# A selective state-space scan on one core: ten columns a state, and the end state's squares moved to VectorE

## What is computed

```
def step(h, inp):
    dA_t, dB_t, x_t, C_t, t = inp
    h = h * dA_t + dB_t * x_t[:, :, None]
    nrm = jnp.sqrt(jnp.sum(h * h, axis=(1, 2), keepdims=True))
    fac = jnp.minimum(20.0 / (nrm + 1e-08), 1.0)
    h = jnp.where(t % 10 == 0, h * fac, h)
    y = jnp.einsum('bdn,bn->bd', h, C_t) + D_param * x_t
    return (h, y)
```

## Time and profile before

| | us |
|---|---|
| median of 3 runs | 1531.29 (1530.69 to 1533.32) |
| the profiled execution, its own time | 1536.68 |
| span of its instructions in the profile | 1534.8 |
| DVE busy / POOL busy / ACT busy / PE busy in the span | 1255.2 / 939.6 / 1121.2 / 1455.1 |

### The profile page before, as it was taken

One profiled execution on the slowest core, in us unless ns is written; L12 is line 12 of the kernel. 1 busy time (PEld: TensorE's weight loads), 2 busy tenths in 40 slices (PEclk: granted clock), 3 DMA queues, 4 the chain that ended last, 5 costly groups with the idle time before them and its releaser, 6 DMA issues.

```text
span 1534.8 us, 25461 instructions
## 1 busy us (share of the span) xinstructions
PE 1455.1 (95%) x6902; PEld 1020.6 (66%) x6902; DVE 1255.2 (82%) x2526; ACT 1121.2 (73%) x2618; POOL 939.6 (61%) x956
## 2 busy tenths in 40 slices
PE   6999999999979999999999999999999998999998
PEld 5555555555467777777777777777666666677776
DVE  6685566745479999999999999999999998788884
ACT  4444455455999999999999999999999964334243
POOL 0224313432269999999999999999999997400000
PEclk9999999999999999999999999999999999999999
DMA  8215437453757667666666666666545447466420
GB/s 269 83 49 176 131 103 198 139 178 115 233 137 208 169 165 188 168 172 167 172 165 181 177 162 181 157 173 172 133 111 112 95 105 224 116 221 193 150 84 28
DMA packets 231557, 236.28 MB, mean 154 GB/s; under 512 B 46040, under 2 KB 197272, under 8 KB 231416
## 3 DMA queue, kind: packets, MB, share of 16 engines
q1 hardware_dynamic: 230472, 233.34, 54.4%
q10 hardware_dynamic: 944, 1.31, 0.2%
HBM read 136.31 MB, written 98.56 MB: 153 GB/s over the span
## 4 chain that ended last, share of the span: by engine, by line
DVE 35%; POOL 14%; PE 12%; issue 5%; DVEq 1%; POOLq 1%; DMA 1%; ACT 0%; SPq 0%; ACTq 0%
DVE h L1346 22%; POOL rc L1110 13%; DVE banks L1336 8%; PE banks L1495 4%; PE banks L1516 3%; PE banks L1526 3%; DVE qs L1330 2%; PE banks L1170 1%; DVEq L1344 1%; DMA ub<-scratch_ub 1%; DVE q_ln_st L1772 1%; DVE q_g L1681 1%; POOLq L1118 1%; DVE q_x L1653 1%; PE banks L1536 0%
## 5 line engine op out<-in xcount | busy, mean ns | idle before, releaser
L1346 DVE TENSOR_TENSOR_SCAN h<-decay,banks 128x352 f32<-128x352 f32 x820 | 710.4, 882 | 57.4 <-DVE banks L1336 2.9
L1121 POOL TENSOR_TENSOR hc<-h,bc 128x640 f32<-128x640 f32 x410 | 593.3, 1447 | 0.0
L1170 PE MATMUL banks<-hc,w_ident 128*128 128x320 f32 (+1 forms) x1664 | 526.6, 440 | 0.1
L1239 ACT ACTIVATE tb<-dtc,a 128x320 f32<-128x320 f32 (+1 forms) x832 | 417.2, 555 | 4.8 <-DVE x L612 4.8
L1170 PEld LDWEIGHTS banks<-hc,w_ident 128*128 128x128 f32 x1664 | 285.0, 191 | 70.7 <-issue 0.8
L1261 ACT ACTIVATE decay<-tb 128x640 f32<-128x640 f32 x410 | 294.9, 723 | 0.0
L1110 POOL TENSOR_TENSOR rc<-qs,w_mhalf 128x1 f32<-128x1 f32 x410 | 225.8, 551 | 110.5 <-DVE qs L1330 110.5
L1156 PE MATMUL banks<-ub 128*128 128x176 f32 x1640 | 273.5, 289 | 2.4 <-DMA ub<-scratch_ub 2.4
L1149 PEld LDWEIGHTS banks<-sc_ss,sc_ones 128*128 128x128 f32 x820 | 123.5, 189 | 158.2 <-ACT sc_sq L1250 152.2
L1156 PEld LDWEIGHTS banks<-ub 128*128 128x128 f32 x1640 | 217.6, 193 | 2.6 <-DMA ub<-scratch_ub 2.6
L1149 PE MATMUL banks<-sc_ss,sc_ones 128*128 128x1 f32 x820 | 151.8, 254 | 37.7 <-ACT sc_sq L1250 19.5
(11 more groups left out here) (133 smaller groups left out, 1818.5 us busy)
## 6 DMA issues: line engine op xcount, KB each, us to landing
ub<-scratch_ub SPq DMA_DIRECT2D x410, 107.5 KB
bc<-scratch_blk SPq DMA_DIRECT2D x205, 160.0 KB, 3.5
scratch_ub<-turned SPq DMA_DIRECT2D x64, 512.0 KB, 3.6
scratch_ub<-spread SPq DMA_DIRECT2D x64, 176.0 KB, 2.6
scratch_xc<-xc SPq DMA_DIRECT2D x8, 1024.0 KB, 4.8
scratch_sg<-sg SPq DMA_DIRECT2D x8, 1024.0 KB, 6.0
piece<-scratch_u SPq DMA_DIRECT2D x32, 256.0 KB, 4.0
q_ys<-scratch_y SPq DMA_DIRECT2D x8, 1024.0 KB, 5.7
```

What stands on the lines that cost most here:

```text
L1121: pool.tensor_tensor(hc[:, pl % 2, :, at * S:(at + 1) * S] .rearrange("p (c b n) e -> p c b n e", c=KE, b=B)[:, :, b], state(m)[:, :, 0:S] ...
L1170: mm = pe.matmul(banks[:, y_bank(p), 0:KE * B * wide], w.ident[:], rhs, start=(n == 0), stop=(n == N - 1))
L1239: act.activation(tanh_rows(c, r), dtc[:, c % 2, k * B:(k + 1) * B, 0:blocks_of(c) * S].rearrange("p b (k e) -> p k b e", e=S), ACT.Tanh, s ...
L1346: dve.tensor_tensor_scan(state(m).rearrange("p r e -> p (r e)")[:, half], decay[:, m % DRING, half], psI[m % B][:, half], 0.0, ALU.mult, A ...
```

## The change

What it does:

- The scan has ten columns a state (W = 10), the ten new steps alone. Column 0 now holds the first new step. To have it, DVE first multiplies the old end state by the decay of that step (`first_step`, L1402, into a new tile `hd`), and `carry` (L1386) then is hd * factor + the input that stands in column 0 of PSUM.
- The decays of first steps come from an extra exp on ACT for four blocks at a time (`first_d`); the exp for each unit has nine columns instead of ten.
- The factors are kept for all blocks (`rcs`), since the last column of a block is not yet scaled when it is read out. `post_stage` scales these columns in a new POOL instruction per tile (`scale_ends`, L1570). The output of step 0 is made apart (`first_output`).
- The squares with their sum, for all but the first two units, move from ACT to DVE (`square`, L1395, a scalar_tensor_tensor with an accumulated output), between carry and the first half scan.
- The halves of the scan are 24 and 40 chains (`LEAD` = 24) instead of 32 and 32, so 240 and 400 columns instead of 352 and 352. The ring of decays has 5 slots instead of 6. PE waits once for the second half scan before a unit's inputs, no longer half by half.

```
-W = S + 1
+W = S
...
-DRING = 6
+DRING = 5
+FG = 4
+LEAD = 24
...
-    HR = NCH // 2
+    HALVES = (slice(0, LEAD), slice(LEAD, NCH))
...
-                if m >= B and c % (KE // 2) == 0:
-                    pe.wait_ge(h_ready[c // (KE // 2)], m + 1)
+                if m >= B and c == 0:
+                    pe.wait_ge(h_ready[1], m + 1)
...
+            if k % FG == 0 and b == 0:
+                if group_of(j) >= 2:
+                    act.wait_ge(hd_ready, (j - (FG if k else (blocks_of(c - 1) - 1) % FG + 1)) * B)
+                dst, src = first_of_group(j)
+                act.activation(dst, src, ACT.Exp, scale=DTA_HALF / SHARP).then_inc(first_ready, 1)
...
-            if m + B < UNITS:
-                squares(act, m + B)
...
         def carry(m):
-            b = m % B
+            j, b = m // B, m % B
+            dve.wait_ge(hd_ready, m + 1)
             dve.wait_ge(norm_ready, m + 1)
             dve.wait_ge(inp_ready, m + 1)
-            dve.tensor_scalar(inp(m)[:, :, 0], state(m - B)[:, :, S], rc[:, b:b + 1], None, ALU.mult
-                              ).then_inc(carry_ready, 1)
+            dve.scalar_tensor_tensor(out=inp(m)[:, :, 0], in0=hd[:, b, :], scalar=rcs[:, j, b:b + 1],
+                                     in1=inp(m)[:, :, 0], op0=ALU.mult, op1=ALU.add).then_inc(carry_ready, 1)
+
+        def square(m):
+            b = m % B
+            for x in range(2):
+                dve.wait_ge(h_ready[x], m + 1)
+            dve.wait_ge(sum_ready, m - B + 1)
+            end = state(m - B)[:, :, W - 1]
+            dve.scalar_tensor_tensor(out=sq[:, b, :], in0=end, scalar=1.0, in1=end, op0=ALU.mult, op1=ALU.mult,
+                                     accum_out=ss[:, b:b + 1]).then_inc(sq_ready, 1)
+
+        def first_step(m):
+            for x in range(2):
+                dve.wait_ge(h_ready[x], m + 1)
+            dve.wait_ge(first_ready, group_of(m // B) + 1)
+            dve.tensor_tensor(hd[:, m % B, :].rearrange("p (g i) -> p g i", i=GR),
+                              state(m - B)[:, :, W - 1].rearrange("p (g i) -> p g i", i=GR),
+                              first_decays(m // B, m % B), ALU.mult).then_inc(hd_ready, 1)
...
+        first_step(0)
         for m in range(UNITS):
             carry(m)
+            if m + 1 < UNITS:
+                if m + 1 >= B:
+                    square(m + 1)
+                first_step(m + 1)
             scan(m, 0)
...
+    def scale_ends(pool, i):
+
+        j0 = -(-i * TT // S)
+        j1 = -(-(i + 1) * TT // S)
+        at = ys[i % 2][:].rearrange("p k (b t) -> p k b t", b=B)[:, :, :, j0 * S - i * TT::S]
+        pool.wait_ge(y_in[i % 2], 16 * (i // 2 + 1))
+        pool.tensor_tensor(at, at, scan.rcs[:, j0:j1].rearrange("p j b -> p b j").unsqueeze(1)
+                           .broadcast_to([P, KE, B, j1 - j0]), ALU.mult).then_inc(scan.ends_scaled, 1)
```

More of the change, by code:

```diff
@@ L700, in vector @@
                 scan.decay_scale(dve)
+                scan.first_output(dve)
                 post.residual_steps(dve)
@@ L808, in scan_stage @@
     qs = own.put("qs", [P, B])
-    rc = own.put("rc", [P, B])
+    rcs = own.put("rcs", [P, NB, B])
+    hd = own.put("hd", [P, B, NCH])
+    c0 = own.put("c0", [P, B, N, 2])
+    s0 = own.put("s0", [P, B])
+    y0 = own.put("y0", [P, KE * B])
     u0 = own.put("u0", [P, KE * B, 2])
@@ L814, in scan_stage @@
     h = second.put("h", [P, 2, B, NCH, W])
+    first_d = second.put("first_d", [P, 2, DB * FG * B * GR])
     hc = second.put("hc", [P, 2, ROWS, QB * S])
@@ L903, in load_first @@
         for b in range(B):
-            sp.dma_start(b0[:, b], dram["bc"][0:N, b:b + 1, 0:2].rearrange("n b t -> b n t")
-                         .broadcast_to([P, N, 2])).then_inc(s_in, 16)
+            for tile, n0 in ((b0, 0), (c0, N)):
+                sp.dma_start(tile[:, b], dram["bc"][n0:n0 + N, b:b + 1, 0:2].rearrange("n b t -> b n t")
+                             .broadcast_to([P, N, 2])).then_inc(s_in, 16)
         sp.wait_ge(blk_out, 32)
@@ L1140, in gpsimd @@
                 spread_b(pool, TILES - 1, m // 4 - 2, m // 4 - 1)
+            if m == UNITS - 17:
+                post.scale_ends(pool, 0)
         weigh(UNITS - 1)
@@ L1249, in squares @@
             act.wait_ge(sum_ready, m - B + 1)
-        act.activation(sq[:, b, :], state(m - B)[:, :, S], ACT.Square,
+        act.activation(sq[:, b, :], state(m - B)[:, :, W - 1], ACT.Square,
                        accum_out=ss[:, b:b + 1]).then_inc(sq_ready, 1)
@@ L1344, in scan @@
                 dve.wait_ge(carry_ready, m + 1)
-            half = slice(x * HR * W, (x + 1) * HR * W)
+            half = slice(HALVES[x].start * W, HALVES[x].stop * W)
             dve.tensor_tensor_scan(state(m).rearrange("p r e -> p (r e)")[:, half], decay[:, m % DRING, half],
@@ L1482, in rstd @@
             pool.tensor_tensor(ln.rs[:], ln.ve[:], w.mhalf[:], ALU.pow).then_inc(ln.rstd_ready, 1)
+        scale_ends(pool, 1)
+        rstd(0)
         for i in range(TILES):
-            rstd(i)
+            if i + 2 < TILES:
+                scale_ends(pool, i + 2)
+            if i + 1 < TILES:
+                rstd(i + 1)
+    def scale_ends(pool, i):
[5 more added lines that the diff above has]
+                           .broadcast_to([P, KE, B, j1 - j0]), ALU.mult).then_inc(scan.ends_scaled, 1)
     def project(pe, i, q, k0, k1):
@@ L1610, in skip @@
         if k == 0:
-            dve.wait_ge(y_in[i % 2], 16 * (i // 2 + 1))
+            dve.wait_ge(scan.ends_scaled, i + 1)
             dve.wait_ge(xc_in[i % 2], 16 * (i // 2 + 1))
@@ L1636, in skip_first @@
         if k == 0:
-            dve.wait_ge(y_in[0], 16)
+            dve.wait_ge(scan.ends_scaled, 1)
         dve.wait_ge(scaled, k + 1)
@@ L1820, in _ @@
                 pre.gpsimd(pool, scan)
-                scan.gpsimd(pool)
+                scan.gpsimd(pool, post)
                 post.gpsimd(pool)
```

73 lines of the change are left out of this document (52 added, 21 removed).

## The result

The changed kernel takes 1901.24 us (median of 4 runs, 1896.34 to 1901.52) and the kernel before 1530.99 (4 runs, 1529.22 to 1533.32). The ratio is 1.2416, with a 95% interval of 1.2397 to 1.2434: 370 us slower, where 1916 us was forecast.

A forecast was written before the change was run, and what follows sets the result against it. VectorE's chain bounds the kernel, POOL's power second. With the square waiting for weigh, 2.25 + 0.01 + 0.08 + 0.11 + 0.10 + 0.57 = 3.12 us a unit against 2.18; 409 x 0.94 = 384 more gives 1921 profiled, 1916 median, range 1815 to 2010.

The forecast's parts named there:

- the full block: Main case: the square behind carry waits on VectorE until POOL's weigh ends; 2.9 to 3.35 us a unit, chance 0.80.
- slips through: Rival: the two short instructions fit into VectorE's 0.47 us wait for carry; 2.01 to 2.13 a unit, around 1490 us, chance 0.06.
- give way early: Rival: weigh has read its inputs before its end, so the square waits 0.23 to 0.9 us; 1540 to 1805 us, chance 0.06.
- PE's clock: Rival: idle gaps drop PE to 1.2 GHz and PE bounds the unit at 3.43 us; some 2040 us, chance 0.07 with still longer.
- Clamp to power 0.28: Unit's first step, from VectorE's clamp to the start of POOL's power: 0.28 us, as before.
- Weigh 1.45: POOL's weigh, with the same 640 elements, takes 1.45 us as before and ends 2.25 us after the clamp.
- From weigh's end to the product 0.01 + 0.08: VectorE behind weigh: next instruction enters at 2.26, 0.01 after weigh's end; the accumulator read adds 0.08 us.
- Product to first half scan 0.11 + 0.10: VectorE's first_step of 64 elements 0.11 us, plus 0.10 for strided reads of the end column by square and product.
- First half scan to clamp 0.57: VectorE's first half scan of 240 columns: 0.80 less 112 columns at 0.00205 us, 0.57 us.
- The short delays: Delays that make a unit 2.18 us on average instead of 2.13; to vanish, as other engines have a us to spare.
- One side remark: ACT's busy time falls by some 200 us and tells nothing.
- half throughput: Skill's rule for scalar_tensor_tensor with two non-bf16 SBUF sources: the square would take 0.07 us more, 27 us over the kernel.

## Why the prediction was right

The mechanism was the one forecast: the full block, a square that ends 0.05 to 0.15 us after weigh, a short product, a carry to first half scan of 1.56 us, about 1 us of waiting before each power, and a granted clock of 1.00 but for the first 60 us of the stage. Experiments that change only one thing show each link: the square alone gives the loss, the wait follows weigh's length, and an operand in PSUM takes it away. The rivals fall. Neither instruction slips through: both are held when they come first. POOL doesn't give way early: the square ends never less than 0.124 after weigh. PE's clock did fall, and PE did bound the unit as that rival has it, but only early in the stage, from 439 to 468 us and briefly at 480; later it was 1.00 in spite of gaps of 1.0 us in each unit. Why it fell at the one place and not at the other stays open. The row that spoke for giving way early stays open too: beside POOL's L277, with one input, a product lost 0.23 us only the earlier trace rows, and no run here tests a one-input instruction of POOL.

The terms, as forecast and as the timeline of the changed kernel has them:

- Clamp to power 0.28, measured 0.20. I wrote that norm loses a wait that was long met, and priced it at nothing; it is worth some 0.07, as in the kernel before without that wait (and, there as here, with the result in another slot).
- Weigh 1.45, measured 1.54. I took the same number of elements for the same time. With ten columns a state the source is one run, and that is the slower form.
- From weigh's end to the product 0.01 + 0.08, measured 0.06. I gave the read of the accumulator a step of 0.08; it has a record of 77 ns, but the next instruction starts together with it (801.36 both), so it costs none. The hand-over is 0.06 instead of 0.01.
- Product to first half scan 0.11 + 0.10, measured 0.18. The stride was priced a little high.
- First half scan to clamp 0.57, measured 0.56.

The sum is 0.20 + 0.52 + 1.54 + 0.06 + 0.18 + 0.56 = 3.06, against 3.12. The two largest misses, -0.08 and +0.09, cancel; that the sum came within 2% is in part luck. The short delays did vanish mostly, as forecast: mean 3.073 to median 3.060, where before it was 2.180 to 2.13. What was left over is 409 x (3.12 - 3.073) = 19 us; of the forecast's 1921 for the profiled execution 1901.5 came. One side remark failed: ScalarE's busy time fell by 74 us (1121.2 to 1046.9) and not by some 200; the gather alone adds 57.

The half throughput of a scalar_tensor_tensor with two SBUF sources, which the Trainium skill states (Vector Engine (DVE) Microarchitecture Reference, Points that are easy to get wrong), would by the estimate have added 0.07 us. The form with accumulation, for which there was no row, has one now: 273 ns with two SBUF operands and 268 with one, so the rule doesn't show at 64 elements.

The rival that put the new instructions into the 0.47 us of VectorE's wait was wrong about the way and also about the price. Where the block is taken away, by an operand in PSUM, the unit is 2.13 with the square on VectorE, no shorter than before, and the rival said 2.0 to 2.13. VectorE then has no idle time: carry 0.18, square and read 0.21, first half scan 0.57, clamp 0.08, product 0.19, second half scan 0.89, 2.12 in all. For carry, square, read and product the rival had 0.41, and they take 0.58. POOL waits 0.06 for each clamp.

## What to carry to other kernels

Before work moves to VectorE, look at where its operands are and at what GpSimd runs at that moment: here two operands in SBUF beside a GpSimd product with two inputs in SBUF cost the rest of that product, though the instruction was 0.27 us long, and with one operand in PSUM it kept its 0.27. A wait of this kind stands in the trace as busy time of the blocked instruction, so compare a record with the shortest of its line before calling an engine busy. When one of two blocked instructions is taken out, the next inherits the wait: count what a cure is worth only with all of them gone.

## What was not expected of the hardware

- With one semaphore fewer ahead of it, and its result in another slot, a POOL instruction started some 0.07 us sooner after its releaser, though that semaphore was long met (0.28 to 0.21 in the kernel before, where it was worth 1%).
- PE's granted clock fell to half early in the scan stage, after waits of 0.93 and 0.83 us and during one of 1.14, and stayed there for 29 us with PE busy throughout (0.50 from 439 to 468 us). Later it was 1.00 beside waits as long.
- POOL's product of 128x640 took 1551 ns with its source in one run and 1447 with ten of every eleven words.
- The read of VectorE's accumulator lasts 77 ns and runs beside the next instruction, at no step of its own.
- ScalarE's exp of 512 elements gathered with a stride took 1112 ns, and of 576 elements in runs of nine 680 ns.
